# Attention's output weights centred beforehand, and the third norm's own centring taken out, in a two-layer model kernel

## The reference, cut to what matters

```
def _layernorm(x, axis=-1, eps=1e-05):
    m = jnp.mean(x, axis=axis, keepdims=True)
    v = jnp.var(x, axis=axis, keepdims=True)
    return (x - m) / jnp.sqrt(v + eps)

# attention: retrieved = what each token reads from a running memory
mu, var = mean and variance of retrieved over the features
normed = (retrieved - mu) / jnp.sqrt(var + 1e-05) * ln_w + ln_b
h = h + x + normed @ Wo + bo          # x is the second norm's output

# experts: x = _layernorm(h)
gate_logits = x @ Wg + bg + bias
topk_vals, topk_idx = top_k(gate_logits, 2);  topk_w = softmax(topk_vals)
combine = one_hot(topk_idx) weighted by topk_w, summed      # token x expert
h1 = relu(einsum('td,edh->teh', x, W1) + b1)
y = einsum('teh,ehd->ted', h1, W2) + b2
h = h + einsum('ted,te->td', y, combine)
```

## Time and profile before

| | us |
|---|---|
| median of 3 runs | 1130.22 |
| lowest and highest | 1129.66, 1130.93 |
| the profiled execution's own time | 1128.81 |
| its span in the profile | 1127.0 |

### The profile page before, as it was taken

One profiled execution on the slowest core, in us unless ns is written; L12 is line 12 of the kernel. 1 busy time (PEld: TensorE's weight loads), 2 busy tenths in 40 slices (PEclk: granted clock), 3 DMA queues, 4 the chain that ended last, 5 costly groups with the idle time before them and its releaser, 6 DMA issues.

```text
span 1127.0 us, 62672 instructions
## 1 busy us (share of the span) xinstructions
PE 1062.1 (94%) x26978; PEld 861.0 (76%) x26978; DVE 695.2 (62%) x3140; ACT 769.3 (68%) x4577; POOL 143.9 (13%) x220
## 2 busy tenths in 40 slices
PE   4799999999999999999999999999798879989998
PEld 2689999999999999999999999999544378823232
DVE  7566455555555555555555554444457679899996
ACT  1466677777777777777777777666568888656664
POOL 4300000001000110001000000000104302321210
PEclk9699999999999999999999999999799989999999
DMA  5000000000000000000000000000000000256777
GB/s 147 7 10 9 9 10 14 9 10 10 9 14 10 9 10 10 11 12 10 10 5 5 5 5 5 5 4 5 3 1 1 1 1 2 87 217 230 257 266 235
DMA packets 30595, 47.22 MB, mean 42 GB/s; under 512 B 12323, under 2 KB 21612, under 8 KB 30317
## 3 DMA queue, kind: packets, MB, share of 16 engines
q1 hardware_dynamic: 29772, 43.08, 11.4%
q10 hardware_dynamic: 544, 0.13, 0.1%
HBM read 40.85 MB, written 2.36 MB: 38 GB/s over the span
## 4 chain that ended last, share of the span: by engine, by line
PE 80%; DVE 11%; ACT 4%; issue 3%; POOL 1%; DMA 0%; SPq 0%; DVEq 0%; ACTq 0%; POOLq 0%
PE bank L681 44%; PE bank L778 7%; PE bank L672 5%; PE bank L761 4%; PE bank L442 3%; PE bank L1748 2%; PE bank L541 2%; PE bank L1694 2%; PE bank L1435 1%; PE bank L1468 1%; PE bank L756 1%; PE bank L1617 1%; PE bank L773 1%; DVE gp L2162 1%; DVE space L2162 1%
## 5 line engine op out<-in xcount | busy, mean ns | idle before, releaser
L681 PE MATMUL bank<-space,whh_hi 128*128 128x32 f16 (+1 forms) x16384 | 575.5, 175 | 8.4 <-DVE space L809 4.6
L681 PEld LDWEIGHTS bank<-space,whh_hi 128*128 128x128 f16 x16384 | 484.0, 96 | 69.0 <-DVE space L809 8.2
L809 DVE TENSOR_TENSOR space<-h_f,space 128x16 f16<-128x16 f32 x2048 | 286.5, 175 | 362.7 <-ACT h_f L790 358.1
L790 ACT ACTIVATE h_f<-bank 128x16 f32<-128x16 f32 x2048 | 294.5, 183 | 224.6 <-PE bank L681 218.7
L796 ACT ACTIVATE space<-bank 128x16 f16<-128x16 f32 x2048 | 291.3, 183 | 1.3 <-PE bank L681 1.3
L672 PE MATMUL bank<-space,whh_lo 128*128 128x32 f16 (+1 forms) x2096 | 131.4, 177 | 0.0
L778 PE MATMUL bank<-space,wih_hi 128*128 128x32 f16 x2048 | 129.1, 177 | 0.0
L761 PE MATMUL bank<-xr,wih_hi 128*128 128x32 f16 x512 | 97.4, 190 | 0.0
L442 PE MATMUL bank<-onehot,tab 128*128 128x128 f16 x448 | 95.5, 219 | 0.5 <-DVE prepare_cur L492 0.5
L756 PE MATMUL bank<-ones,bias 128*128 128x32 bf16 x512 | 91.6, 179 | 0.0
L672 PEld LDWEIGHTS bank<-space,whh_lo 128*128 128x128 f16 x2096 | 90.0, 96 | 0.0
(11 more groups left out here) (309 smaller groups left out, 1602.6 us busy)
## 6 DMA issues: line engine op xcount, KB each, us to landing
space<-weights_kept SPq DMA_DIRECT2D x64, 512.0 KB, 8.0
space<-in_x SPq DMA_DIRECT2D x28, 129.0 KB, 3.1
out<-res SPq DMA_DIRECT2D x7, 256.0 KB, 9.9
space<-in_wrec SPq DMA_DIRECT2D x1, 768.0 KB, 4.4
space<-in_wx SPq DMA_DIRECT2D x1, 744.5 KB, 9.2
brec<-in_brec SPq DMA_DIRECT2D x1, 260.0 KB
ew<-in_ew SPq DMA_DIRECT2D x1, 256.0 KB, 4.0
weights_kept<-wturned SPq DMA_DIRECT2D x8, 32.0 KB, 1.8
```

The source lines that it names most:

```text
L681: mm = pe.matmul(own[:, m, 0:copies, :], w[:, k, m * P:(m + 1) * P], state[:, k, :].unsqueeze(1).to_broadcast([P, copies, B]), start=False ...
L790: act.activation(h_f[layer][:, s % 2, :, :], own, ACT.Tanh, scale=scale[layer]).then_inc(s_h[layer], 1)
L809: dve.tensor_tensor(h[layer][:, :, s % RINGS[layer], 1, :], h_f[layer][:, s % 2, :, :], h[layer][:, :, s % RINGS[layer], 0, :], ALU.subtra ...
```

## The change

The output weights are centred once, during the recurrent layer, so that what attention adds to `res` has mean zero in columns 0 to 63; a 65th column of weights gives the sum, which goes into column 64 of `res`. The bias row `cwb` gets the same treatment. Then the third norm needs neither `third_mean` nor `third_centre`, and `mean_back` goes: the mean in column 64 is sent along with the gate weights as a ninth row, and the bias product (L1742) adds it with a ninth row of 1/64 in `eb2`. The attention product is now 130 wide for each pair of tiles, 520 columns in all, which don't fit in one bank: they now begin at column 252 of bank 6 and end at column 260 of bank 7. The three early steps of PE in bank 6 wait for `att_scaled` (the scaling of the product by DVE) where they waited for `att_variance`. `gate_pairs` on POOL waits for `gates_shifted` (after L2090) where it waited for `gates_biased` (after L2085).

```diff
+        def centred_weights(dve, link, i):
+            rows = slice((i + 1) % 2 * D, ((i + 1) % 2 + 1) * D)
+            own = wobd[rows, (i + 1) % 2, :]
+            if i == 0:
+                link(dve.reduce_sum(wsum[:, :], wobd[:, :, 0:D], AX.XY))
+            elif i < 3:
+                link(dve.scalar_tensor_tensor(own[:, 0:D], wsum[rows, :].to_broadcast([D, D]), -1.0 / D, own[:, 0:D],
+                                              ALU.mult, ALU.add))
+            else:
+                link(dve.tensor_copy(own[:, D:D + 1], wsum[rows, :]))
...
+            elif k == 3 and 20 <= o < 25:
+                centred_weights(dve, link, o - 20)
...
+        att_out = banks[3][:, 252:252 + TT * (D + 1)]
...
             def gate_pairs(x):
-                pool.wait_ge(s_lg, x + 1)
+                pool.wait_ge(s_lm, x + 1)
...
             def third_square(x):
                 act.wait_ge(s_xc, B + x + 1)
-                act.activation(sq[:, :, :], xc[:, :, :], ACT.Square, scale=D ** -0.5).then_inc(s_sq, 1)
+                act.wait_ge(s_var, B + x)
+                act.activation(sq[:, :, :], res[:, span(x), 0:D], ACT.Square, scale=D ** -0.5).then_inc(s_sq, 1)
...
             def gate_exp(x):
+                if x:
+                    act.wait_ge(s_wgt_t, x)
                 act.wait_ge(s_lm, x + 1)
+                act.activation(gleft[:, NE, :], res[:, span(x), D], ACT.Copy)
                 act.activation(gex[:, :, :], gc[:, :, :], ACT.Exp).then_inc(s_ex, 1)
...
                 for i in range(4):
-                    mm = pe.matmul(bank[7][:, i * P:(i + 1) * P], ntb[:, i * P:(i + 1) * P], wobd[:, :],
+                    mm = pe.matmul(att_out[:, i * 2 * (D + 1):(i + 1) * 2 * (D + 1)], ntb[:, i * P:(i + 1) * P],
+                                   wobd[:, :, :].rearrange("p h d -> p (h d)"),
...
                 if b == 4:
-                    pe.wait_ge(s_sd, b)
+                    pe.wait_ge(s_wor, b)
                     third_turn(pe, bank[6], 0)
                 elif b == 5:
-                    pe.wait_ge(s_sd, b)
+                    pe.wait_ge(s_wor, b)
                     gates(0, bank[6][:, D:2 * D])
                 read(b)
                 if b == 6:
-                    pe.wait_ge(s_sd, b)
-                    weights_turned(0, bank[6][0:NE * TT, P:2 * P])
+                    pe.wait_ge(s_wor, b)
+                    weights_turned(0, bank[6][0:(NE + 1) * TT, P:2 * P])
...
             def add_out(b):
-                own, part = res[:, span(b), 0:D], tmp8[:, :, 0:D]
-                link(dve.tensor_tensor(own, own, rows(cwb[:, :]), ALU.add))
+                own, part = res[:, span(b), :], tmp8[:, :, :]
+                link(dve.tensor_tensor(own, own, cwb.unsqueeze(1).to_broadcast([P, TT, D + 1]), ALU.add))
                 dve.wait_ge(s_rs, b + 1)
-                dve.tensor_tensor(part, tokens(bank[7][:, :]), spread(stat[:, 7, :]), ALU.mult).then_inc(s_wor, 1)
+                dve.tensor_tensor(part, tokens(att_out), stat[:, 7, :].unsqueeze(2).to_broadcast([P, TT, D + 1]),
+                                  ALU.mult).then_inc(s_wor, 1)
...
             dve.wait_ge(s_row_k, 1)
+            link(dve.reduce_sum(stat[:, 0, 0:1], cwb[:, 0:D], AX.X))
+            link(dve.scalar_tensor_tensor(cwb[:, 0:D], stat[:, 0, 0:1].to_broadcast([P, D]), -1.0 / D, cwb[:, 0:D], ALU.mult,
+                                          ALU.add))
+            link(dve.tensor_tensor(cwb[:, D:D + 1], cwb[:, D:D + 1], stat[:, 0, 0:1], ALU.add))
             for b in range(B):
...
                 if n == 0:
                     add_out(B - 1)
-                elif n in (1, 2):
-                    mean_back(n - 1)
+                    third_variance(2)
                 if y + 1 < B:
                     if step == 2:
                         gate_logits(y + 1, bank[6][:, 0:TT * NE])
+                        if y + 2 < B:
+                            third_variance(y + 2)
...
                 if y + 2 < B:
-                    if step == 0:
-                        third_mean(y + 2)
-                    elif step == 1:
-                        third_centre(y + 2)
-                    elif step == 3:
-                        third_variance(y + 2)
-                    elif step == 4:
-                        mean_back(y + 2)
-                    elif step == 5:
+                    if step == 5:
                         third_scale(y + 2)
...
+    eb2[NE] = 1.0 / D
```

More of the change, by code:

```diff
@@ L199, in build @@
         s_lnb = sem("norm_bias_spread")
[L200 to L201 removed]
+        s_wo, s_sd, s_rs, s_wor = (sem(n) for n in ("att_projected", "att_variance", "att_rstd", "att_scaled"))
         s_gt, s_lg, s_rank, s_lm, s_ex, s_wgt, s_wgt_t, s_wgt_c, s_wgt_out, s_wgt_rows = (
@@ L896, in build @@
         nrmw = tmp("nrmw", [P, TT, D + 1])
[L897 removed]
+        nrm = nrmw[:, :, 0:D]
         sq = tmp("sq", [P, TT, D])
@@ L1263, in _ @@
             act.wait_ge(s_row_b, 1)
-            act.activation(cwb[:, :], bank[6][:, D:2 * D], ACT.Copy).then_inc(s_row_k, 1)
+            act.activation(cwb[:, :], bank[6][:, D:2 * D + 1], ACT.Copy).then_inc(s_row_k, 1)
             for b in range(2):
@@ L1358, in _ @@
                 if step == 0 and y < B:
-                    weights_copy(y, bank[6][0:NE * TT, P:2 * P])
+                    weights_copy(y, bank[6][0:(NE + 1) * TT, P:2 * P])
                 if step == 1 and y + 1 < B:
                     third_copy(y + 1, bank[3])
-                elif step == 2 and y + 2 < B:
-                    third_square(y + 2)
+                    if y + 2 < B:
+                        third_square(y + 2)
                 elif step == 4 and y + 1 < B:
@@ L1741, in second @@
                     for half in range(2):
-                        mm = pe.matmul(sum_bank(b)[half * D:(half + 1) * D, :], eb2[0:NE, :],
+                        mm = pe.matmul(sum_bank(b)[half * D:(half + 1) * D, :], eb2[0:NE + 1, :],
                                        weight_rows[:, half * 512:(half + 1) * 512], start=True, stop=False,
@@ L2044, in add_out @@
             def add_out(b):
-                own, part = res[:, span(b), 0:D], tmp8[:, :, 0:D]
-                link(dve.tensor_tensor(own, own, rows(cwb[:, :]), ALU.add))
+                own, part = res[:, span(b), :], tmp8[:, :, :]
+                link(dve.tensor_tensor(own, own, cwb.unsqueeze(1).to_broadcast([P, TT, D + 1]), ALU.add))
                 dve.wait_ge(s_rs, b + 1)
-                dve.tensor_tensor(part, tokens(bank[7][:, :]), spread(stat[:, 7, :]), ALU.mult).then_inc(s_wor, 1)
+                dve.tensor_tensor(part, tokens(att_out), stat[:, 7, :].unsqueeze(2).to_broadcast([P, TT, D + 1]),
+                                  ALU.mult).then_inc(s_wor, 1)
                 dve.wait_ge(s_wor, b + 1)
-                link(dve.tensor_tensor(own, own, part, ALU.add))
+                dve.tensor_tensor(own, own, part, ALU.add).then_inc(s_xc, 1)
             dve.tensor_scalar(lnb[:, :], ones32[:, :], column(LN_B), None, ALU.mult).then_inc(s_lnb, 1)
             per = lambda x: x.unsqueeze(2).to_broadcast([P, TT, NE])
[L2055 to L2061, removed]
-            def mean_back(x):
-                own = res[:, span(x), :]
-                link(dve.scalar_tensor_tensor(own[:, :, 0:D], spread(own[:, :, D]), 1.0 / D, own[:, :, 0:D], ALU.mult,
-                                              ALU.add))
             def third_variance(x):
@@ L2074, in third_scale @@
                 dve.wait_ge(s_xs, OPEN + B + x)
-                dve.tensor_tensor(nrm[:, :, :], xc[:, :, :], spread(stat[:, 4, :]), ALU.mult).then_inc(s_nrm, 1)
+                dve.tensor_tensor(nrm[:, :, :], res[:, span(x), 0:D], spread(stat[:, 4, :]), ALU.mult).then_inc(s_nrm, 1)
             def third_low(x):
@@ L2107, in gate_weights @@
                     dve.wait_ge(s_wgt_t, x)
-                dve.tensor_tensor(gleft[:, :, :].rearrange("p e t -> p t e"), gc[:, :, :], per(gst[:, 2, :]),
+                dve.tensor_tensor(gleft[:, 0:NE, :].rearrange("p e t -> p t e"), gc[:, :, :], per(gst[:, 2, :]),
                                   ALU.mult).then_inc(s_wgt, 1)
@@ L2132, in _ @@
                     add_out(b - 1)
-                if b == 1:
-                    third_mean(0)
-                    third_centre(0)
-                elif b == 2:
+                if b == 2:
                     third_variance(0)
@@ L2139, in _ @@
                     third_scale(0)
-                    third_mean(1)
-                elif b == 4:
-                    third_centre(1)
                 elif b == 5:
@@ L2147, in _ @@
                     third_scale(1)
-                elif b == 7:
-                    third_mean(2)
-                    third_centre(2)
                 if b < B - 1:
```

24 lines of the change are left out of this document (13 added, 11 removed).

## The result

| | before | after |
|---|---|---|
| median of 20 runs, us | 1130.71 | 1132.53 |
| lowest and highest | 1129.25, 1132.22 | 1129.28, 1136.79 |
| ratio, 95% interval | | 1.0019 (1.0011 to 1.0028) |
| profiled execution, its span | 1128.81, 1127.0 | 1130.24, 1128.4 |

The changed kernel is 1.8 us slower by the medians. That is within the 0.2% that the prediction calls "same", but it isn't nothing: the interval leaves out 1, and a repetition on another chip gave 1.0030 (1.0017 to 1.0044). The forecast was 1131.0, in a range of 1126.8 to 1134.6.

What follows compares the result with a forecast made beforehand. PE's order bounds the attention loop, DVE the expert rounds until PE binds. Entry +7.0, head -3.8, rounds -5.6 make -2.4; clock +2.2 and +1.0 make +0.8: profile 1129.6, median 1131.0, range 1126.8 to 1134.6.

Steps and rivals of the forecast that it cites:

- The wait in b = 4: Attention loop: PE's turn waits for DVE's scaling until 957.3 instead of starting at 951.89, PE idle for 4.7 us.
- Up to the expert loop: Attention loop, b = 4 to 6: new waits make the entry into the expert loop 7.0 us later, bounds +4.9 and +8.5.
- the signs that I named (4 to 5, about 7): Attention loop: ACT's eviction of b = 4 comes 4 to 5 us later relative to the loop's first, b = 5 about 7.
- Clock: PE's clock falls behind the new waits: +2.2 us for b = 4, +1.0 for further falls up to the expert loop's head.
- rival B: Stall multiplies: second clock fall in b = 5 (+2.0) and one at the expert loop's head (+1.65), 1133.7 us; chance 0.22.
- Head of the expert loop: Before the first bias product: DVE loses three `mean_back` (-2.15) and the half clock goes (-1.65), together -3.8 us.
- Five rounds: Expert loop, 1009.06 to 1094.66: DVE's round falls to 15.1, PE binds at 16.0, 80.0 instead of 85.6, -5.6 us.
- rival D: Expert loop: waits for rows from DRAM take back perhaps half of each round's gain, +3.5 us, 1134.5; chance 0.06.
- Rival C: Attention loop: the new waits don't bite, as the scaling comes before PE reaches the turn, -8.7 us, 1121.5; chance 0.07.
- Priced at nothing: Parts counted as free, among them five small DVE instructions in the recurrent layer, at most 1.1 us, 0.3 kept.
- POOL's collision: Expert loop: POOL's moved `gate_pairs` lies beside `third_variance` and the next `mult`, costing DVE +0.47 a round, or about 0.6.
- the sign of 1.6 to 1.8: Expert loop: the DVE `mult` behind `third_variance` would take 1.6 to 1.8 us.

Runs made afterwards that it cites:

- fill3: Changed kernel plus products nobody reads in PE's waits of b = 4 (17), b = 5 (8) and b = 6 (6): 1129.09 us, 0.9996 of the kernel before.
- bank0: Changed kernel with PE's three early steps written to bank 0 instead of bank 6, not waiting for the scaling: 1122.34 us, 0.9928 of the kernel before.
- pairs_lm: Kernel before with one part of the change alone, POOL's differences starting after the gates' shift (L2090): 1128.33 us, 0.9985 of the kernel before.
- fill: Changed kernel plus products nobody reads in PE's waits of b = 4 (17) and b = 5 (8): 1133.89 us, 1.0027 of the kernel before.
- pairs_lg: Changed kernel with POOL's differences moved back beside the gates' shift: 1132.13 us, 1.0023 of the kernel before.

## Why the prediction was right, step by step

- *The wait in b = 4.* Forecast: turn at 957.3 plus what the loop starts later. Measured 958.09, with the first keys 0.81 later than before: 957.28. Idleness 4.65 for a forecast 4.7. The bias row, 0.7 of it, shows as 44.54 - 43.97 = 0.6, in one profile of each.
- *Up to the expert loop.* Forecast without clock +7.0, of which 0.7 lie ahead of the loop: 6.3 from scores to turned weights. fill3, in which the clock holds, has 30.99 against 24.96: +6.0. Its evictions come 9.41 and 20.78 behind the scores of b = 4, where before they came 5.29 and 14.35 behind: +4.1 and +6.4, and the forecast without the 0.7 was +4.1 and +6.4. In after itself they are +6.0 and +9.5; the signs that I named (4 to 5, about 7) left the clock out, and failed by that.
- *Clock.* Forecast +2.2 and +1.0. The stage from scores to turned weights grew by another 34.09 - 30.99 = 3.1, by the fall at 957 to 962 and the second at 974. So half of rival B came true, the second fall in the attention loop, but both falls together cost 3.1, the forecast's price, and not B's 4.2. The other half did not: the head of the expert loop stayed at full clock.
- *Head of the expert loop.* Forecast -3.8, measured 34.10 - 30.24 = -3.9.
- *Five rounds.* Forecast 80.0, measured 80.4. DVE has 14.99 in a round for a forecast 15.1. One round, from the third to the fourth bias product, took 16.4. DVE waited 0.42 and 1.06 for rows from DRAM around its start (the second is shown), and the chain that ended last runs through such a row there, so a row is the likely cause. In the other rounds such waits, 0.90 the longest, held nothing: rival D fell. Rival C's 1121.5 is what bank0 measured to 0.8, as a kernel of its own.

```profile
1032.12 1.23 DVE L2165 TENSOR_TENSOR gel<-gel,space 128x1024 f32<-128x1024 f32 x1 [1.06 <-DMA space<-weights_kept]
```

- *Priced at nothing.* Here is the error: five instructions in a layer that PE fills stood in the sum at nothing (the 0.3 kept for them was not added) and cost 0.3 to 0.5. The start of the loop was 0.8 later, but by the 2.2 between two profiles of one kernel, 0.8 can be chance. The forecast of 1129.6 for the profile was 0.6 low. The median stands 2.3 above the profiled execution, where I added 1.4 from before: the times of the changed kernel have a longer tail (six of 20 are at 1134.97 or above), which a single profile doesn't show, and fill3 has none. So the median, 1132.53, is at the upper edge of the forecast's own range (1129.0 to 1132.6).
- *POOL's collision.* Forecast +0.47 for the product, with about 0.6 as the other figure, for which the prediction shows no working. Measured where the reduction lies between: 0.24 in pairs_lm, and 0.26 in after (1.48 at 1061.48), so that the sign of 1.6 to 1.8 failed. It is worth nothing in the time of after, since PE binds.

## What to carry to other kernels

A product that grows by a few columns over the edge of a PSUM bank takes over the other tenants of the next bank: look who writes there and for what event they will now wait, before counting the work that is saved. A wait in an engine's queue costs what is behind it, not what it guards; moving the early work to a bank that is free kept the whole gain (7.8 us, then 11.4 with the small steps moved). Before filling PE's waits to hold its clock, list all of them: with the two longest filled and the third left open, the fall came behind the third and the time did not improve; with all three filled the time fell by 3 us.

## What was not expected of the hardware

A GpSimd instruction that starts 0.16 behind a DVE product of two SBUF inputs took 1.95 instead of 1.04, and the DVE product nothing; one that starts 0.10 ahead took its 1.04, and the product 2.02 instead of 1.22. POOL and DVE in after:

```profile
1093.00 1.04 POOL L1104 TENSOR_TENSOR gdiff<-lg 128x512 f32<-128x512 f32 x1 [12.40 <-DVE gc L2098]
```

```profile
1093.10 2.02 DVE L2165 TENSOR_TENSOR gel<-gel,space 128x1024 f32<-128x1024 f32 x1 [0.18 <-DMA space<-weights_kept]
```

The clock fell behind a wait of only 1.44 (fill) once the longer ones ahead were filled, and behind one of 1.19 in pairs_lg, where the same instructions with the same wait left it at full speed in after.
